# Delta rule of a two-layer network: the residual formed by VectorE per head, instead of by VectorE and GpSimd in turn

## The chip, the cores and the metric

The kernel runs on one core of one Trainium2 chip. The metric is the device time of one execution in microseconds (us). The kernel before took 2767.0 us, the median of 3 runs (2761.95 to 2785.57).

The engines' names in the profile: PE is TensorE's matmul, PEld its weight load, DVE is VectorE, ACT is ScalarE, POOL is GpSimd and SP is the engine that starts most transfers.

## The reference, cut to what matters

The network has two layers, each an attention block and a mixture of experts with adaptive layer norm. Only the attention block of the second layer is touched, a gated delta rule with 16 value heads of 64 by 64 over 8 sequences of 512 tokens:

```python
def step(S, xs):
    q_t, k_t, v_t, g_t, b_t = xs
    S = S * jnp.exp(g_t)[..., None, None]
    kv = jnp.einsum('bhk,bhkv->bhv', k_t, S)
    S = S + jnp.einsum('bhk,bhv->bhkv', k_t, (v_t - kv) * b_t[..., None])
    o_t = jnp.einsum('bhk,bhkv->bhv', q_t, S)
    return (S, o_t)
```

Ahead of it, q, k and v are projected, put through a causal convolution of 4 taps and a SiLU, and q and k are normalised. Behind it, the output is normalised per head, multiplied by silu(z) and projected.

## The kernel before, in words

The function delta1 computes the block in chunks of 32 tokens. The 128 partitions hold 4 sequences by 32 tokens, and the 8 sequences go in two passes of 16 chunks, so there are 32 steps k, and 16 pairs m of two steps (an even step e = 0, an odd step e = 1). The heads of a step are worked on in two halves f = 0 and 1, each a tile of 128 x 512 (8 heads by 64).

A step k does this, with the line and the engine of each part:

- read_out (PE, L2454): keys times state into the bank BK[f], then queries times state into BQ[f]. DVE scales BK[f] by the decay and key norm gk into Xs (L2086), and BQ[f] by the decay gT into O (L2092).
- residual (POOL, L1998): Xs becomes v - Xs, in place. The values vt come from PE (L2431) through ACT's SiLU (L2306).
- solve (PE, L2487): the triangular inverse Tt times Xs into BK[f]; ACT copies that to Ws (L2318).
- weigh (POOL, L2019): Ud is Ws times the decay to the chunk's end. add_state (PE, L2504): keys times Ud into BK. decay (POOL, L2010): the state S times its decay, one instruction for each f. update (DVE, L2189): S minus BK, two instructions for each f.
- attend (PE, L2518) and accumulate (DVE, L2195): O minus the weighted part of the chunk.

The signs are those of Tt and Pt, which are built from minus beta (d32 is minus the identity).

Beside that runs work for other chunks. For four steps ahead: the projection (PE, L2415), whose taps ACT makes (L2271, L2276, L2282: raw, the bank BY and yp) and DVE adds up (L2137, L2138, L2141), two times a step, as long as k is below 28. For the pair ahead: the norms (PE L2404, ACT L2257, DVE L2119 to L2132), POOL's diagonal Lt (L1992), DVE's scan L2149 and products L2156 and L2159 (even steps), and the forward substitution of the chunk's triangular system, 30 rows of a product (L2173) and a sum (L2174) on DVE, each chained to the one before through a semaphore, 11 of them in even steps and 19 in odd ones. For the step behind: the output's squares (ACT L2251, DVE L2099), the factor (DVE L2106 and L2107, ACT L2263, DVE L2112 and L2113), ACT's L2325, POOL's gate L2026, transposes and the output product (PE L2527, L2534).

Each engine's program is written out in a fixed order by hand, in a loop over k that runs the functions above one after another, and semaphores join them. Nothing is scheduled by a tool. DVE's order in a step is: squares, read_out of both halves, first convolution, squares, total, then in even steps norms and attend, in odd steps substitution; second convolution; and so on to accumulate and update of half 0, more substitution, and the same of half 1. POOL's order is: window, residual of both halves, diag (even steps), decay of half 0, diag (even), weigh of both halves, initial (even), decay of half 1, gated, halo.

decay(k, f) waits only for both of PE's read-outs of the step (the semaphore p_qs), and in the program stands behind the residuals:

```python
def decay(k, f):
    ...
    pool.wait_ge(s["p_qs"], half(k, 1))
```

Of the kernel before, what the change touches and what calls it, by code (L numbers as in the profile page):

```python
# [7 lines left out]
ALU = mybir.AluOpType  # L8
# [24 lines left out]
HV, HK, DK = 16, 8, 64  # L33
# [10 lines left out]
def bcast(ap, axis, n):  # L44

    a = [list(x) for x in ap.ap]
    a.insert(axis, [0, n])
    return bass.AP(ap.tensor, ap.offset, a)
# [1811 lines left out]
def delta1(nc, g, a):  # L1860

    PB, X, ident = g["PB"], g["X"], g["ident"]
    V, G = nc.vector, nc.gpsimd
    NS = 2 * NCK
    NP = NS // 2
    HF = HV // 2
    with ExitStack() as keep:
# [6 lines left out]
        Wqk, Wcv, Wz, Wo, cw, hT, bT, gT, GC = [w[n] for n in ("Wqk", "Wcv", "Wz", "Wo", "cw", "hT", "bT", "gT", "GC")]  # L1874
        with Stage(nc, ["p_ks", "p_qs", "p_w", "p_ds", "p_pu", "p_kk", "p_m",
                        "v_ks", "v_qs", "v_s", "v_o", "v_lt", "v_at", "v_ac", "v_tt", "v_conv", "v_ss",
                        "v_rn", "v_sr", "v_link", "g_x", "g_s", "g_d1", "g_t", "g_t0", "g_halo", "g_on", "g_hw", "g_ac", "v_nm", "a_kq", "g_ud",
                        "a_m", "a_w", "a_yp", "a_on", "a_sq", "a_osq", "a_or", "a_lk", "d_al0", "d_al1", "d_out"]) as s:
            raw = s.sb("raw", [P, 4, 2, 4, KS - 1 + 2 * CK])
            hw = s.sb("hw", [P, 2, KS, 4, CK])  # L1880
# [6 lines left out]
            gk = s.sb("gk", [P, 2, 2, HV])  # L1887
# [3 lines left out]
            vt = s.sb("vt", [P, 2, 512])  # L1891
            zs = s.sb("zs", [P, 2, 512])
            O = s.sb("O", [P, 2, 2, 512])
# [14 lines left out]
            Xs = s.sb("Xs", [P, 2, 512])  # L1908
# [5 lines left out]
            BK = (PB[3], PB[4])  # L1914
            BQ = (PB[5], PB[6])
            BY = PB[7]
            hd = lambda x: x.rearrange("p (h d) -> p h d", d=DK)
# [20 lines left out]
            done = lambda kind, x: USE[(kind, x)] + 1  # L1938
            half = lambda k, f: 2 * k + f + 1
            updates = lambda k, f: 2 * (k - k // NCK) + f + 1  # L1940

            with nc.Block() as block:
# [29 lines left out]
                def _(pool):  # L1972
# [5 lines left out]
                    def window(k):  # L1978
                        if k >= 2:
                            pool.wait_ge(s["p_m"], done("z", 2 * (k - 2) + 1))  # L1980
                        h = hb(k // NCK)
                        at = CK * (k % NCK)
                        last = None
                        for i in range(KS):
                            last = G.tensor_copy(hw[:, k % 2, i, :, :], h[:, :, at + i:at + i + CK])  # L1985
                        last.then_inc(s["g_hw"], 1)

                    def diag(c):
                        if c:
                            pool.wait_ge(s["v_at"], c)  # L1990
                        pool.wait_ge(s["v_nm"], c // 2 + 1)
                        G.tensor_tensor(Lt[:, :, :], bcast(bk[:, c % 2, :], 2, CK), bcast(w["d32"][:, :], 1, HV), ALU.mult)\  # L1992
                            .then_inc(s["g_d1"], 1)

                    def residual(k, f):
                        pool.wait_ge(s["v_ks"], half(k, f))
                        pool.wait_ge(s["a_m"], done("v", 2 * k + f))
                        G.tensor_tensor(Xs[:, f, :], vt[:, f, :], Xs[:, f, :], ALU.subtract).then_inc(s["g_x"], 1)  # L1998

                    def decay(k, f):  # L2000
                        if k == NS - 1:
                            return
                        pool.wait_ge(s["p_qs"], half(k, 1))
                        Sf = S[:, 2 * f:2 * f + 2, :, :]
                        if k % NCK == NCK - 1:
                            G.memset(Sf, 0.0).then_inc(s["g_s"], 1)
                        else:
                            gc = GC[:, k // NCK, k % NCK, 2 * f:2 * f + 2, :, :].rearrange("p x q v -> p (x q v)")
                            S3 = Sf.rearrange("p x q (v d) -> p (x q v) d", d=DK)
                            G.tensor_tensor(S3, S3, bcast(gc, 2, DK), ALU.mult).then_inc(s["g_s"], 1)  # L2010
# [11 lines left out]
                    def gated(k):  # L2022
                        for f in range(2):
                            pool.wait_ge(s["a_m"], done("z", 2 * k + f))
                            pool.wait_ge(s["a_on"], half(k, f))
                            G.tensor_tensor(O[:, k % 2, f, :], O[:, k % 2, f, :], zs[:, f, :], ALU.mult)\  # L2026
                                .then_inc(s["g_on"], 1)
# [24 lines left out]
                    for k in range(FIRST, LAST):  # L2052
                        m, e = k // 2, k % 2
                        if 0 <= k + 1 < NS:
                            window(k + 1)
                        if 0 <= k < NS:
                            residual(k, 0)
                            residual(k, 1)
                        if 0 <= m + 1 < NP and e == 0:
                            diag(2 * (m + 1))  # L2060
                        if 0 <= k < NS:
                            decay(k, 0)
                        if 0 <= m + 1 < NP and e == 0:
                            diag(2 * (m + 1) + 1)
                        if 0 <= k < NS:
                            weigh(k, 0)
                            weigh(k, 1)
                        if 0 <= m + 1 < NP and e == 0:
                            initial(m + 1)
                        if 0 <= k < NS:  # L2070
                            decay(k, 1)
                        if 0 <= k - 1 < NS:
                            gated(k - 1)
                        if (k + 4) // 2 < NP:
                            halo(2 * (k + 4))
                            halo(2 * (k + 4) + 1)

                @block.vector
                def _(dve):
                    link = linker(dve, s["v_link"])  # L2080

                    def read_out(k, f):
                        dve.wait_ge(s["p_ks"], half(k, f))
                        if k:
                            dve.wait_ge(s["p_w"], half(k - 1, f))
                        V.tensor_tensor(hd(Xs[:, f, :]), hd(BK[f][:, :]),  # L2086
                                        bcast(gk[:, k // 2 % 2, k % 2, HF * f:HF * f + HF], 2, DK), ALU.mult)\
                            .then_inc(s["v_ks"], 1)
                        dve.wait_ge(s["p_qs"], half(k, f))
                        if k >= 2:  # L2090
                            dve.wait_ge(s["p_m"], done("ot", 2 * (k - 2) + f))
                        V.tensor_tensor(hd(O[:, k % 2, f, :]), hd(BQ[f][:, :]), cols(gT, k, f), ALU.mult)\  # L2092
                            .then_inc(s["v_qs"], 1)
# [88 lines left out]
                    def update(k, f):  # L2182
                        if k % NCK == NCK - 1:
                            return
                        dve.wait_ge(s["p_ds"], updates(k, f))
                        dve.wait_ge(s["g_s"], half(k, f) + 2)
                        for x in (2 * f, 2 * f + 1):
                            Sx = S[:, x, :, :].rearrange("p q n -> p (q n)")
                            last = V.tensor_tensor(Sx, Sx, BK[x % 2][:, :], ALU.subtract)  # L2189
                        last.then_inc(s["v_s"], 1)  # L2190

                    def accumulate(k, f):
                        dve.wait_ge(s["p_pu"], half(k, f))
                        dve.wait_ge(s["v_qs"], half(k, f))
                        V.tensor_tensor(O[:, k % 2, f, :], O[:, k % 2, f, :], BQ[f][:, :], ALU.subtract)\  # L2195
                            .then_inc(s["v_o"], 1)

                    for k in range(FIRST, LAST):
# [6 lines left out]
                        if here:  # L2205
                            read_out(k, 0)
                            read_out(k, 1)
# [36 lines left out]
                def _(act):  # L2244
# [57 lines left out]
                    def values(k, f):  # L2302
                        act.wait_ge(s["p_m"], done("v", 2 * k + f))
                        if k:
                            act.wait_ge(s["g_x"], half(k - 1, f))
                        A_(vt[:, f, :], M[USE[("v", 2 * k + f)] % 2][:, :], ACT.Silu).then_inc(s["a_m"], 1)  # L2306

                    def gate(k, f):
# [76 lines left out]
                def _(pe):  # L2385
# [94 lines left out]
                    def solve(k, f):  # L2480
                        if k % 2 == 0 and f == 0:
                            pe.wait_ge(s["v_tt"], k // 2 + 1)
                        pe.wait_ge(s["g_x"], half(k, f))
                        for h in range(HF):
                            for x in range(4):
                                rows = slice(CK * x, CK * x + CK)
                                last = mm(BK[f][rows, DK * h:DK * h + DK], Tt[rows, :, k % 2, HF * f + h],  # L2487
                                          Xs[rows, f, DK * h:DK * h + DK], start=True, stop=True,
                                          tile_position=(CK * x, CK * x))
                        last.then_inc(s["p_w"], 1)  # L2490
# [118 lines left out]
```

## Time and profile before

| what | value |
| --- | --- |
| median of 3 runs | 2767.0 us (2761.95 to 2785.57) |
| the profiled execution | 2778.46 us |
| its span, first to last instruction | 2776.8 us |
| steps of the delta rule within it | about 1239 to 2324 us |
| busy over the span | PE 2194.6 us (79%), DVE 1890.6 (68%), ACT 1435.8 (52%), POOL 769.1 (28%) |
| mean granted TensorE clock | 0.854 |

A timeline row reads: start in us, duration in us, engine, line, operation, output <- inputs, shape, count, and in brackets how long the engine had been idle before it and what ended that. Rows that stand together on an engine are merged, with their count (x4) and the time from the first start to the last end. A row of the groups by line has busy us, mean ns of one, and the idle time before them. The share of busy time over the span says little here, since the stages have different limits; what counts for the change is the stretch of the delta rule.

### The profile page before, as it was taken

How to read it: one execution, taken by the hardware profiler on the slowest of the kernel's cores; microseconds unless marked ns; L12 is line 12 of the kernel's file. 1: busy time of each engine (PE TensorE's matmuls, PEld its weight loads, DVE VectorE, ACT ScalarE, POOL GpSimd, SP SyncE). 2: the span in 40 equal slices, each digit the busy share in tenths (PEclk: the TensorE clock that was granted, in tenths of full speed). 3: DMA queues.
4: the chain of work that ended last, by engine and by line, in shares of the span. 5: the costliest groups of instructions: out<-in, count | busy, mean ns of one | idle time of the engine just before them, and what ended most of it. 6: DMA issues, size and time to landing. Idle time of an engine off the chain costs nothing. (4 is left out here: it accounts for less than half of the span.)

```text
span 2776.8 us, 63709 instructions
## 1 busy us (share of the span) xinstructions
PE 2194.6 (79%) x25656; PEld 1388.4 (50%) x25656; DVE 1890.6 (68%) x4429; ACT 1435.8 (52%) x2901; POOL 769.1 (28%) x845
## 2 busy tenths in 40 slices
PE   2698888889888493468888888888888886587984
PEld 1244444444444282146666666666666664365552
DVE  2477677777766325568888898888888883673433
ACT  0376667667666221255666666666666644132321
POOL 1000001000010141024444444344444442202884
PEclk8599899999887796668888988888888888597997
DMA  5000000000000042200000000000000000433334
GB/s 187 26 1 5 5 5 9 5 5 8 5 7 6 25 117 53 65 9 11 12 12 12 12 12 12 12 12 11 11 12 12 4 4 6 139 110 91 53 43 86
DMA packets 109526, 85.53 MB, mean 31 GB/s; under 512 B 22366, under 2 KB 97282, under 8 KB 108976
## 3 DMA queue, kind: packets, MB, share of 16 engines
q1 hardware_dynamic: 95664, 68.31, 8.4%
q0 software_dynamic: 13568, 13.14, 2.9%
q8 instruction: 203, 3.33, 0.5%
q14 instruction: 91, 0.75, 0.1%
HBM read 59.22 MB, written 22.71 MB: 30 GB/s over the span
## 5 line engine op out<-in xcount | busy, mean ns | idle before, releaser
L617 ACT ACTIVATE Pr<-Pr,nmax 128x512 f32<-128x512 f32 x512 | 341.2, 714 | 177.4 <-DVE nmax L552 175.3
L722 PE MATMUL bank<-ident,Pr 128*128 128x128 f32 x2048 | 315.5, 297 | 71.6 <-DVE PT L561 59.8
L722 PEld LDWEIGHTS bank<-ident,Pr 128*128 128x128 f32 x2048 | 242.1, 151 | 258.8 <-DVE PT L561 157.2
L552 DVE CUSTOM_DVE_ANT_0 Pr<-bank,Tb 128x512 f32<-128x512 f32 x512 | 331.0, 684 | 42.4 <-PE bank L708 42.3
L561 DVE COPY PT<-bank 128x512 f32<-128x512 f32 x256 | 176.4, 689 | 188.2 <-PE bank L736 184.0
L2431 PE MATMUL bank<-Wcv,hw 128*128 128x512 f32 x512 | 265.1, 665 | 8.8 <-POOL hw L1985 5.3
L2173 DVE TENSOR_TENSOR pr<-AC,Tc 128x30 f32<-128x30 f32 (+14 forms) x480 | 214.9, 448 | 16.9 <-POOL Tc L2049 3.6
L624 ACT ACTIVATE PT<-bank 128x512 f32<-128x512 f32 x256 | 151.0, 590 | 112.9 <-PE bank L736 83.3
L2174 DVE TENSOR_TENSOR Tc<-Tc,pr 128x30 f32<-128x30 f32 (+14 forms) x480 | 178.8, 373 | 16.5
L708 PE MATMUL bank<-kp,qp 8*128 8x512 f32 x1024 | 178.4, 696 | 1.1 <-DVE nmax L552 1.1
L2431 PEld LDWEIGHTS bank<-Wcv,hw 128*128 128x128 f32 x512 | 103.5, 214 | 125.8 <-issue 118.0
L2282 ACT ACTIVATE yp<-raw,cwq 128x256 f32<-128x256 f32 x384 | 160.1, 510 | 0.0
L736 PE MATMUL bank<-PT,vp 128*9 128x512 f32 x1024 | 154.4, 676 | 0.0
L1998 POOL TENSOR_TENSOR Xs<-vt,Xs 128x512 f32<-128x512 f32 x64 | 80.6, 1275 | 243.7 <-DVE Xs L2086 243.6
L432 POOL DMA_INDIRECT disp<-H,slot x32 | 31.9, 995 | 396.8 <-DVE slot L508 389.5
L423 POOL TENSOR_SCALAR H<-X,rs,nm 128x128 f32<-128x128 f32 x32 | 14.0, 454 | 412.7 <-DVE nm L540 412.7
L2325 ACT ACTIVATE O<-O,nrm 128x64 f32<-128x64 f32 x512 | 125.4, 335 | 4.1 <-DVE nrm L2113 3.9
L2504 PE MATMUL bank<-Ud,Kt 32*64 32x128 f32 x1920 | 74.1, 296 | 56.1 <-DVE S L2189 51.7
L2487 PE MATMUL bank<-Xs,Tt 32*32 32x64 f32 x4096 | 88.5, 246 | 34.4 <-POOL Xs L1998 34.3
L2010 POOL TENSOR_TENSOR S<-S,GC 128x1024 f32<-128x1024 f32 x60 | 114.4, 1907 | 0.0
L1507 POOL DMA_INDIRECT acc<-eo,ids x64 | 101.0, 1578 | 40.6 <-issue 18.6
L2318 ACT ACTIVATE Ws<-bank 128x512 f32<-128x512 f32 x64 | 38.1, 596 | 139.9 <-PE bank L2487 139.8
(398 smaller groups left out, 4533.6 us busy)
## 6 DMA issues: line engine op xcount, KB each, us to landing
aB<-alpha SPq DMA_DIRECT2D x64, 128.0 KB, 2.7
Tb<-scores SPq DMA_DIRECT2D x1, 7168.0 KB
w<-in_L_ffn_W SPq DMA_DIRECT2D x16, 256.0 KB, 5.2
rawW<-in_L_ffn_up_w SPq DMA_DIRECT2D x16, 256.0 KB, 3.1
rawW<-in_L_ffn_gw SPq DMA_DIRECT2D x16, 256.0 KB, 3.5
rawW<-in_L_ffn_down_w SPq DMA_DIRECT2D x16, 256.0 KB, 4.0
disp<-zero SPq DMA_DIRECT2D x1, 2580.0 KB, 15.5
xin<-disp SPq DMA_DIRECT2D x8, 322.5 KB, 6.3
```

What stands on the lines that cost most here:

```text
L552: V.tensor_tensor_reduce(out=Pr[:, s, i, :], in0=pS[hh][:, :], in1=Tb[:, h, at:at + L], scale=-1.0, scalar=3.0e38, op0=ALU.add, op1=ALU.mi ...
L561: V.tensor_copy(PT[:, m % NPS, :], pT[m % 2][:, :]).then_inc(r["b_evd"], 1)
L617: A_(Pr[:, s, i, :], Pr[:, s, i, :], ACT.Exp, scale=-1.0, bias=nmax[:, s, i:i + 1])\
L624: A_(PT[:, m % NPS, :], pT[m % 2][:, :], ACT.Copy).then_inc(r["b_eva"], 1)
L708: mm(pS[hh][:, :], qp[rows, G % SLOTS, i * P:(i + 1) * P], kp[rows, G % SLOTS, :], start=True, stop=True, tile_position=(32 * hh, 0)).then ...
L722: last = TR(pT[m % 2][:, t * P:(t + 1) * P], Pr[:, (G % 2) * HG + hh, t, j * P:(j + 1) * P], ident[:, :])
L736: mm(pO[32 * hh:32 * hh + HD0 + 1, :], vp[:, b % 2, j, G % NG * HG + hh, :], PT[:, m % NPS, :], start=(j == 0), stop=(j == LT - 1), tile_p ...
L2173: link(V.tensor_tensor(o, bcast(AC[:, i + 1:CK, i], 2, i), bcast(Tc[:, i, 0:i], 1, n), ALU.mult))
L2174: link(V.tensor_tensor(Tc[:, i + 1:CK, 0:i], Tc[:, i + 1:CK, 0:i], o, ALU.add))
L2282: last = A_(yp[:, i, j, :, :], raw[:, tp, j, :, i:i + 2 * CK], ACT.Copy, scale=tap(j, i))
L2325: last = A_(of, of, ACT.Copy, scale=nrm[:, k % 2, HF * f + h:HF * f + h + 1])
L2431: last = mm(o[:, :], tokens(k, i), Wcv[:, i, 512 * f:512 * f + 512], start=(i == 0), stop=(i == KS - 1))
```

## The change

Before, the residual takes two operations on two engines: DVE's product of BK[f] and gk (128x512, gk broadcast along the 64 elements of each head), then POOL's difference v - Xs. After, DVE does both at once with scalar_tensor_tensor, whose scalar is one value per partition. Since the factor gk differs from head to head, each half takes 8 such instructions of 128x64. They form gk * BK - v, minus the former residual, so the two places that subtracted what follows from it (L2189 and L2195) now add. POOL's function and its semaphore g_x go; ACT's values and PE's solve wait for v_ks in its place, and DVE waits for the values before it starts.

```diff
-                    def residual(k, f):
-                        pool.wait_ge(s["v_ks"], half(k, f))
-                        pool.wait_ge(s["a_m"], done("v", 2 * k + f))
-                        G.tensor_tensor(Xs[:, f, :], vt[:, f, :], Xs[:, f, :], ALU.subtract).then_inc(s["g_x"], 1)
-
...
-                        if 0 <= k < NS:
-                            residual(k, 0)
-                            residual(k, 1)
...
-                        V.tensor_tensor(hd(Xs[:, f, :]), hd(BK[f][:, :]),
-                                        bcast(gk[:, k // 2 % 2, k % 2, HF * f:HF * f + HF], 2, DK), ALU.mult)\
-                            .then_inc(s["v_ks"], 1)
+                        dve.wait_ge(s["a_m"], done("v", 2 * k + f))
+                        for h in range(HF):
+                            of = slice(DK * h, DK * h + DK)
+                            last = V.scalar_tensor_tensor(Xs[:, f, of], BK[f][:, of],
+                                                          gk[:, k // 2 % 2, k % 2, HF * f + h:HF * f + h + 1],
+                                                          vt[:, f, of], ALU.mult, ALU.subtract)
+                        last.then_inc(s["v_ks"], 1)
...
-                            last = V.tensor_tensor(Sx, Sx, BK[x % 2][:, :], ALU.subtract)
+                            last = V.tensor_tensor(Sx, Sx, BK[x % 2][:, :], ALU.add)
...
-                        V.tensor_tensor(O[:, k % 2, f, :], O[:, k % 2, f, :], BQ[f][:, :], ALU.subtract)\
+                        V.tensor_tensor(O[:, k % 2, f, :], O[:, k % 2, f, :], BQ[f][:, :], ALU.add)\
...
-                            act.wait_ge(s["g_x"], half(k - 1, f))
+                            act.wait_ge(s["v_ks"], half(k - 1, f))
...
-                        pe.wait_ge(s["g_x"], half(k, f))
+                        pe.wait_ge(s["v_ks"], half(k, f))
```

The order on DVE in an odd step, before, from the squares' reduction ahead of read_out to the first convolution behind it (nrm holds the squares' sums, bank is here BK or BQ, and BY in the last row):

```order
1993 L2099 TENSOR_REDUCE nrm<-osq 128x8
1994 L2086 TENSOR_TENSOR Xs<-bank,gk 128x512
1995 L2092 TENSOR_TENSOR O<-bank,gT 128x512
1996 L2086 TENSOR_TENSOR Xs<-bank,gk 128x512
1997 L2092 TENSOR_TENSOR O<-bank,gT 128x512
1998 L2137 TENSOR_TENSOR bank<-bank,yp 128x512
```

The same place on DVE after the change:

```order
1993 L2095 TENSOR_REDUCE nrm<-osq 128x8
1994 L2081 SCALAR_TENSOR_TENSOR Xs<-bank,gk,vt 128x64 x8
1995 L2088 TENSOR_TENSOR O<-bank,gT 128x512
1996 L2081 SCALAR_TENSOR_TENSOR Xs<-bank,gk,vt 128x64 x8
1997 L2088 TENSOR_TENSOR O<-bank,gT 128x512
1998 L2133 TENSOR_TENSOR bank<-bank,yp 128x512
```

Nothing else changes its place on DVE; each L2086 has become 8 instructions. PE's and ACT's orders are as before.

The order on GpSimd in the same odd step, before: the window of the next step (hw), the residuals (Xs), decay of half 0 (S), weigh (Ud), decay of half 1, gate (O).

```order
146 L1985 COPY hw<-hTa 128x128 x4
147 L1998 TENSOR_TENSOR Xs<-vt,Xs 128x512 x2
148 L2010 TENSOR_TENSOR S<-S,GC 128x1024
149 L2019 TENSOR_TENSOR Ud<-Ws,dl 128x512 x2
150 L2010 TENSOR_TENSOR S<-S,GC 128x1024
151 L2026 TENSOR_TENSOR O<-O,zs 128x512 x2
```

The same place on GpSimd after the change:

```order
141 L1985 COPY hw<-hTa 128x128 x4
142 L2005 TENSOR_TENSOR S<-S,GC 128x1024
143 L2014 TENSOR_TENSOR Ud<-Ws,dl 128x512 x2
144 L2005 TENSOR_TENSOR S<-S,GC 128x1024
145 L2021 TENSOR_TENSOR O<-O,zs 128x512 x2
```

The decay of half 0 now stands directly behind the window. In an even step the diagonal Lt (L1992), which waits for DVE's norms, stands between the two, before and after.

## Rows read from the trace of the kernel before

**Rows 1.** Stretches: length, busy PE, PEld, DVE, ACT, POOL; PEclk, DMA share, GB/s.
```profile
1579.09:1605.68 26.59, 24.05 (x368) 17.79 (x368) 23.84 (x49) 16.28 (x41) 10.61 (x13) 0.87 0.02 5
...
1646.20:1677.36 31.16, 28.82 (x368) 21.26 (x368) 24.18 (x50) 16.32 (x41) 11.25 (x14) 0.73 0.02 4
1677.36:1717.82 40.46, 33.56 (x801) 22.59 (x800) 38.74 (x72) 30.37 (x73) 18.32 (x19) 1.00 0.06 17
1717.82:1748.93 31.11, 28.81 (x368) 21.29 (x368) 24.19 (x50) 16.30 (x41) 11.60 (x14) 0.73 0.02 4
```

**Rows 2.** Waits of DVE, 1239 to 2324 us: total us, times, longest.
```profile
DVE bank L2137 <- ACT yp L2282: 42.0, 14, 3.2
DVE rkq L2119 <- ACT rkq L2257: 22.2, 14, 2.8
```

**Rows 3.** Timeline of an odd step, from the read-out on.
```profile
1696.44 3.31 PE L2454 MATMUL bank<-S,kq 64*32 64x128 f32 x128
...
1700.74 0.68 DVE L2086 TENSOR_TENSOR Xs<-bank,gk 128x512 f32<-128x512 f32 x1
1701.34 0.68 DVE L2092 TENSOR_TENSOR O<-bank,gT 128x512 f32<-128x512 f32 x1
1701.50 2.50 POOL L1998 TENSOR_TENSOR Xs<-vt,Xs 128x512 f32<-128x512 f32 x2 [8.67 <-DVE Xs L2086]
...
1702.82 1.14 PE L2487 MATMUL bank<-Xs,Tt 32*32 32x64 f32 x64 [2.01 <-POOL Xs L1998]
...
1703.95 1.92 POOL L2010 TENSOR_TENSOR S<-S,GC 128x1024 f32<-128x1024 f32 x1
...
1705.31 0.81 ACT L2276 ACTIVATE bank<-bank,cwq 128x256 f32<-128x256 f32 x2 [0.20 <-DVE yc L2141]
...
1705.81 1.06 POOL L2019 TENSOR_TENSOR Ud<-Ws,dl 128x512 f32<-128x512 f32 x1
1705.91 0.98 DVE L2106 TENSOR_TENSOR rq<-rkq 128x8 f32<-128x8 f32 x1
...
1706.93 0.17 DVE L2107 TENSOR_TENSOR nrm<-nrm,rq 128x16 f32<-128x16 f32 x1
```

**Rows 4.** The same odd step's second half.
```profile
1713.63 1.91 POOL L2010 TENSOR_TENSOR S<-S,GC 128x1024 f32<-128x1024 f32 x1
...
1714.63 0.94 DVE L2113 TENSOR_TENSOR nrm<-nrm,rkq 128x16 f32<-128x16 f32 x1
...
1717.82 1.28 DVE L2189 TENSOR_TENSOR S<-S,bank 128x512 f32<-128x512 f32 x2
...
1719.24 1.98 PE L2504 MATMUL bank<-Ud,Kt 32*64 32x128 f32 x32 [3.38 <-DVE S L2189]
```

**Rows 5.** The even step behind it.
```profile
1731.77 0.69 DVE L2086 TENSOR_TENSOR Xs<-bank,gk 128x512 f32<-128x512 f32 x1
...
1737.39 0.17 DVE L2106 TENSOR_TENSOR rq<-rkq 128x8 f32<-128x8 f32 x1
...
1739.19 0.35 DVE L2119 RECIPROCAL rkq<-rkq 128x32 f32<-128x32 f32 x1 [1.43 <-ACT rkq L2257]
...
1741.11 1.90 POOL L2010 TENSOR_TENSOR S<-S,GC 128x1024 f32<-128x1024 f32 x1
1741.19 2.90 DVE L2149 TENSOR_TENSOR_SCAN Lt<-aB,Lt 128x512 f32<-128x512 f32 x1 [0.98 <-POOL Lt L1992]
...
1742.70 1.94 PE L2487 MATMUL bank<-Xs,Tt 32*32 32x64 f32 x64
...
1748.93 0.70 DVE L2137 TENSOR_TENSOR bank<-bank,yp 128x512 f32<-128x512 f32 x1 [3.17 <-ACT yp L2282]
```

**Rows 6.** scalar_tensor_tensor elsewhere: two groups by line.
```profile
L1631 DVE SCALAR_TENSOR_TENSOR hid<-bank,biasT,sg 128x512 f32<-128x512 f32 x64 | 48.0, 750 | 55.7 <-PE bank L1554 55.7
L1128 DVE SCALAR_TENSOR_TENSOR Y<-Y,factor,gbr 128x128 f32<-128x128 f32 x32 | 9.1, 344 | 11.4 <-DMA Y<-y 11.4
```

**Rows 7.** Timeline: four of L1128 in a row.
```profile
1065.22 1.14 DVE L1128 SCALAR_TENSOR_TENSOR Y<-Y,factor,gbr 128x128 f32<-128x128 f32 x4 [11.38 <-DMA Y<-y]
```

More of the change, by code:

```diff
@@ L1876, in delta1 @@
                         "v_ks", "v_qs", "v_s", "v_o", "v_lt", "v_at", "v_ac", "v_tt", "v_conv", "v_ss",
-                        "v_rn", "v_sr", "v_link", "g_x", "g_s", "g_d1", "g_t", "g_t0", "g_halo", "g_on", "g_hw", "g_ac", "v_nm", "a_kq", "g_ud",
+                        "v_rn", "v_sr", "v_link", "g_s", "g_d1", "g_t", "g_t0", "g_halo", "g_on", "g_hw", "g_ac", "v_nm", "a_kq", "g_ud",
                         "a_m", "a_w", "a_yp", "a_on", "a_sq", "a_osq", "a_or", "a_lk", "d_al0", "d_al1", "d_out"]) as s:
```

## The prediction

> **What bounds the kernel now.** I read four views: busy time by stretch, the waits of VectorE (DVE), the timeline of one pair of steps, and the groups by line for durations. The change touches only the delta rule, 32 steps k = 0 to 31 between 1239 and 2324 us. Its work repeats with a period of two steps: an even step carries the attention part (L2119 to L2164), an odd one most of the substitution.
>
> The busy time by stretch [rows 1] splits one period in two. From 1677.36 to 1717.82, from the second convolution of an even step to the first state update of the odd one, DVE is busy 38.74 of 40.46 us, and the gaps of 0.04 us between its chained operations (1705.91 + 0.98 to 1706.93, [rows 3]), some 40 of them, fill the rest: it waits for nobody. From 1717.82 to 1748.93 (31.11 us) DVE is busy only 24.19 us, while TensorE (PE) is busy 28.81. There the path runs over PE: the last row of [rows 4] shows PE waiting 3.38 us for the state update L2189, and then PE hardly stops through keys, gates, output, read-out, norms, similarities and solve, until ScalarE (ACT) has made yp. DVE waits for that at L2137, 3.17 us [rows 5]. Over the loop, DVE's waits [rows 2] are 42.0 us in 14 waits for yp (3.0 on average at a longest of 3.2, so nearly all periods are alike) and 22.2 in 14 for the roots (L2119).
>
> So the cycle is 40.5 us of DVE work plus some 31 us of PE work. What DVE gets more of in the first part is paid in full, in the second it is free up to its waits. The odd step's read_out (1700.74, [rows 3]) lies in the first part, the even step's (1731.77) in the second.
>
> **What the change adds: eight small operations for one.** Before, L2086 takes 0.68 us, and the next operation starts 0.60 after it [rows 3]. No row shows a 128x64 scalar_tensor_tensor from PSUM. Two rows bound it [rows 6, 7]: L1631, the same operation on 512 elements from PSUM, takes 750 ns, and L1128, on 128 elements from SBUF, 344. That is (750 - 344) / 384 = 1.06 ns an element, so 64 elements take 344 - 68 = 0.28 us. Four L1128 in a row span 1.14 us [rows 7], so their starts are (1.14 - 0.344) / 3 = 0.265 apart; less 64 elements that is 0.20 us. The lower end of the cost is then 8 x 0.20 = 1.60 against 0.60, +1.0 us per half and +2.0 per step. The upper end is no overlap at all, 0.32 us each with the 0.04 that stands between chained operations: 2.56 against 0.60, +2.0 per half and +3.9 per step. I take the lower, because four operations of this very kind, with their scalar read from memory, overlap in L1128's row.
>
> The Trainium skill, "VectorE: DVE Perf Modes", section "The DRAIN you can't avoid", says the next Vector operation does not start until the pipe has emptied, which would give the upper end. The trace disagrees where nothing holds the operation (starts 0.60 apart at 0.68 us each), and the page allows for that itself.
>
> **Even steps: hidden.** The 2.0 us fall between read_out and L2119, where DVE waits for the roots, 1.43 us in this period and 22.2 / 14 = 1.6 on average. The rest, about 0.5, goes into the 3.17 us wait for yp. Neither of these two arrivals depends on the read-out's DVE part: solve(k, 0) starts at 1742.70 [rows 5], and Xs is ready 8 us before. Cost 0; if that cover were gone it would be 2.0 us a step.
>
> **Odd steps: paid.** The first convolution L2137 starts 2.0 us later. That also moves ACT, whose L2276 waits for its result (1705.31, [rows 3]), and through yp, the table loads and Ws it moves GpSimd's weigh(k, 1) and decay(k, 1) by 2.0.
>
> **What the change removes.** GpSimd's L1998, 2 x 1.25 us a step. It ran next to DVE operations that read PSUM, and these were not slowed (0.68 us each), so its own time was free. What waited for it was PE's solve(k, 0), at 1702.82 after 2.01 us. The new Xs is ready at 1700.74 + 7 x 0.20 + 0.28 = 1702.42, against 1702.82: 0.3 to 0.4 us earlier, but PE then waits for DVE's L2189 anyway, so this is worth nothing. What is late next there is DVE itself.
>
> **Who meets whom.** DVE operations with two SBUF inputs stand still while GpSimd works: L2106, two inputs of 8 elements, takes 0.98 us beside GpSimd's L2019 (1705.81) and 0.17 in the even step [rows 3, 5]; the scan L2149 takes 2.90 beside decay. Without the residual, decay(k, 0) of an odd step starts when PE's read-out ends (1696.44 + 3.31 = 1699.75) instead of at 1703.95, and lies beside a reduction and the new operations. Weigh(k, 0) starts at about 1704.3, beside PSUM operations. So L2106's 0.81 us go. But decay of half 1, at 1713.63 [rows 4], moves by 2.0 with weigh ahead of it, where DVE would have moved only by 1.2: decay then covers 1715.65 to 1717.55, and L2113, which reads two SBUF tiles, comes at 1715.83 instead of after half of decay is over. It would take 1.7 us instead of the 0.94 of [rows 4], and the 0.8 are lost again. Net: +2.0 us for an odd step.
>
> **The sum.** 14 odd steps (k = 1 to 27) by 2.0 = 28, and two (k = 29, 31), where no convolution is left and DVE is not full, at 1 each: +30 us. The profiled execution took 2778.46 us (span 2776.8); it would become 2808.5. It lies 11.5 above the median of the three runs, 2767.0, so against the median I forecast 2797 us (+1.1%).
>
> **Rivals.**
>
> 1. *Part of it comes back.* Should L2113 not meet decay(k, 1), because ACT catches up, an odd step costs 1.2: 14 x 1.2 + 2 = 19 us. PE's stretch depends also on the clock: 31.16 and 31.11 us at 0.73 granted, but 26.59 at 0.87 [rows 1], levels of 1.2 and 2.4 GHz mixed. The periods so far vary with that, and shifting the pattern by 2 us may give more short stretches. One such in each four periods would give 4.5 x 3.5 = 16 back. For it: rows of both kinds exist. Against it: the waits for yp [rows 2] are nearly all alike. Time 2782 (+8 to +22 us).
>
> 2. *The clock turns it round: faster.* If the changed rhythm held the clock near 0.87 in every PE stretch, that stretch would shrink to DVE's own work. That is 31.11 - 3.17 - 1.43 = 26.5 us, plus the read-out's 2.0: 28.5, so 2.6 us less per period, against 2.0 more. 14 x (-0.6) is -9 us; with L2113 free as well it is 14 x (-1.4) = -20 us: 2750. It decides from a mean stretch below 29.1 us. For it speaks only the one short stretch of [rows 1]; against it, that PE idles no less than before in the DVE stretch.
>
> 3. *The new operations stand still beside decay.* They read PSUM, one SBUF tile and a scalar from SBUF. If the scalar counts as a second SBUF input, those of half 0 wait for decay(k, 0) to end, about 1.3 us after read_out starts: 14 x 3.3 + 2 = +48 us, 2815. The Trainium skill, "GPSIMD Engine Reference", section "Specifications", names two SBUF inputs (or a 2-port mode) as what contends with GpSimd; the stalled L2106 and L2149 agree, and whether a scalar counts it doesn't say. No row has this operation beside GpSimd's arithmetic.
>
> 4. *No overlap.* At 3.9 us a step the odd ones cost 14 x 3.9 + 2 = 57 us, 2824; even steps still hide it in 1.5 + 3.17.
>
> That the change doesn't do what it says is no rival: the order shows GpSimd without the subtraction and DVE with 8 operations at each of 64 places.
>
> **How the numbers follow.** Forecast 0.44 (its own range 2790 to 2804); rival 1 0.26; rival 2 0.08; rival 3 0.12; rival 4 0.10. A measurement tells about 1% from no change, here 27.7 us, so the line is at 2794.7. Of the forecast's case two thirds lie above it, a third below; rivals 3 and 4 are slower; rival 1 is within; of rival 2 a third or so would be faster by over 1%. Slower 0.29 + 0.22 = 0.51, same 0.15 + 0.26 + 0.05 = 0.46, faster 0.03. The range goes from inside rival 1 to rival 4: 2774 to 2828.
>
> **What would show it.** Right: the 8 operations span 1.7 us, and starts within are 0.20 apart; the DVE stretch of a period becomes 42.5; the even step's wait for the roots is near 0 and the one for yp stays above 2 us; L2106 near 0.17 in odd steps, and L2113 near 1.7; GpSimd 80 us less busy. Wrong: starts 0.3 apart (rival 4); a first new operation of over 1 us in odd steps (rival 3); a DVE stretch under 42 (the meeting with decay); PE stretches whose mean is not near 31 (rival 1 or 2).

## The result, and the profile after

The changed kernel takes 2807.22 us, the median of 4 runs (2801.45 to 2814.16), against 2770.49 us for the kernel before (4 runs). The ratio is 1.0109, with a 95% interval of 1.0074 to 1.0143: about 30 us slower by the ratio, 37 by the medians, where 2797 us (+30) was forecast. In the profiled executions, of which the one after is the lowest of its four, the difference is smaller: 2801.45 against 2778.46 us (span 2799.7 against 2776.8, +22.9). Each execution has its own pattern of the granted TensorE clock, as shown below.

The busy time by engine, from the page of the profile after:

```profile
PE 2200.4 (79%) x25656; PEld 1396.3 (50%) x25656; DVE 1937.1 (69%) x4877; ACT 1434.9 (51%) x2901; POOL 691.4 (25%) x781
```

POOL is 78 us less busy than before, DVE only 47 us more. Its Xs operations, 448 instructions more, take 103.5 us instead of 43.5, and the rest of its groups together some 13 us less.

The odd step that answers to [rows 3] and [rows 4], from the timeline:

```profile
1705.53 2.00 POOL L2005 TENSOR_TENSOR S<-S,GC 128x1024 f32<-128x1024 f32 x1 [7.04 <-PE bank L2450]
...
1706.41 1.62 DVE L2081 SCALAR_TENSOR_TENSOR Xs<-bank,gk,vt 128x64 f32<-128x64 f32 x8
...
1707.95 0.68 DVE L2088 TENSOR_TENSOR O<-bank,gT 128x512 f32<-128x512 f32 x1
...
1708.09 1.63 PE L2483 MATMUL bank<-Xs,Tt 32*32 32x64 f32 x64 [1.60 <-DVE Xs L2081]
1708.54 1.62 DVE L2081 SCALAR_TENSOR_TENSOR Xs<-bank,gk,vt 128x64 f32<-128x64 f32 x8
...
1710.67 0.69 DVE L2133 TENSOR_TENSOR bank<-bank,yp 128x512 f32<-128x512 f32 x1
...
1712.86 0.81 ACT L2272 ACTIVATE bank<-bank,cwq 128x256 f32<-128x256 f32 x2 [2.00 <-DVE yc L2137]
1713.45 0.17 DVE L2102 TENSOR_TENSOR rq<-rkq 128x8 f32<-128x8 f32 x1
...
1720.17 1.04 POOL L2014 TENSOR_TENSOR Ud<-Ws,dl 128x512 f32<-128x512 f32 x1 [8.70 <-ACT Ws L2314]
...
1721.18 1.90 POOL L2005 TENSOR_TENSOR S<-S,GC 128x1024 f32<-128x1024 f32 x1
...
1721.36 1.75 DVE L2109 TENSOR_TENSOR nrm<-nrm,rkq 128x16 f32<-128x16 f32 x1
```

Eight operations span 1.62 us, and the first convolution comes 4.26 us after the read-out's start (1706.41 to 1710.67). Decay now starts at 1705.53, right behind PE's read-out, and lies over the first eight. L2102 takes 0.17 us, where it had taken 0.98 [rows 3]; L2109 takes 1.75 beside the second decay, where it had taken 0.94 [rows 4].

The stretches that answer to [rows 1] (length; busy PE, PEld, DVE, ACT, POOL; granted clock): a PE stretch, the DVE stretch behind it, the next PE stretch.

```profile
1655.26:1683.02 27.76, 25.26 (x367) 18.74 (x368) 25.07 (x63) 15.55 (x39) 7.14 (x11) 0.82 0.02 5
1683.02:1725.36 42.34, 35.55 (x802) 23.48 (x800) 40.62 (x86) 30.99 (x76) 17.45 (x20) 0.96 0.05 16
1725.36:1756.88 31.52, 28.98 (x366) 21.93 (x367) 25.32 (x63) 15.54 (x39) 9.07 (x12) 0.68 0.02 4
```

The DVE stretch has grown from 40.46 to 42.34 us, and DVE is still busy through it; over 12 periods its mean went from 40.58 to 42.48. The PE stretches alternate: in the 12 periods between steps 1 and 27 in which both ends can be read, four last about 28 us and eight 31.4 to 31.6. Their mean, 30.3 us, is next to the 30.5 of the same periods before.

The even step behind it, which answers to [rows 5]:

```profile
1738.98 1.63 DVE L2081 SCALAR_TENSOR_TENSOR Xs<-bank,gk,vt 128x64 f32<-128x64 f32 x8 [0.32 <-PE bank L2450]
1741.12 1.62 DVE L2081 SCALAR_TENSOR_TENSOR Xs<-bank,gk,vt 128x64 f32<-128x64 f32 x8
...
1747.15 0.35 DVE L2115 RECIPROCAL rkq<-rkq 128x32 f32<-128x32 f32 x1 [0.74 <-ACT rkq L2253]
...
1750.66 1.94 PE L2483 MATMUL bank<-Xs,Tt 32*32 32x64 f32 x64
...
1756.88 0.70 DVE L2133 TENSOR_TENSOR bank<-bank,yp 128x512 f32<-128x512 f32 x1 [3.16 <-ACT yp L2278]
```

The read-out is 1.9 us longer here too. The wait for the roots takes up 0.7 of it (1.43 to 0.74). Some 0.3 go because the read-out comes sooner behind the odd step's state update (13.62 us instead of 13.95), and the stretch is 0.4 longer, at a granted clock of 0.68 instead of 0.73. The wait for yp is whole. Over the loop, the waits that answer to [rows 2]:

```profile
DVE bank L2133 <- ACT yp L2278: 31.6, 13, 3.2
...
DVE rkq L2115 <- ACT rkq L2253: 6.6, 9, 1.7
```

22.2 us for the roots have become 6.6, and 42.0 for yp 31.6. The two waits are 26 us less, where DVE got 14 x 1.9 = 26.6 us more work in the even steps. That the two agree so well is partly chance: in the eight long PE stretches the wait for yp is whole (3.16 us each, as before), and most of what is gone of it is gone in the four short ones, where it is 0.7 to 1.3 us, as it was 0.78 in the one of 26.59 us before [rows 1].

Where the loop's time went, from step starts (the first Xs operation of each step): from step 0 to step 31 it took 1107.45 us against 1083.54, +23.9. The 14 odd steps from 1 to 27 are 23.2 us longer, the 13 even ones from 2 to 26 2.2, steps 28 to 30 together 2.8, and step 0 is 4.2 shorter. Of the odd steps' 23.2, step 15 has 4.3 alone. It is the last of the first pass and has no state update. 2.4 us of it are waits for ACT and PE that the profile before does not have there, and that even_only's has without any change in that step. The other 13 are 1.46 us longer each, in four parts:

| part of an odd step, mean of 13 | before | after |
| --- | --- | --- |
| read-out to first convolution | 2.39 | 4.26 |
| to the second convolution (with L2106's meeting) | 9.15 | 8.34 |
| to the state update (with L2113's meeting) | 5.61 | 6.35 |
| to the even step's read-out | 13.86 | 13.52 |

In the last part GpSimd's gate of O meets fewer substitution rows, which take some 0.4 us each when nothing holds them. These are the ones that it stretches, two before and one after:

```profile
1719.01 0.89 DVE L2173 TENSOR_TENSOR pr<-AC,Tc 128x220 f32<-128x220 f32 x1
...
1720.36 1.44 DVE L2173 TENSOR_TENSOR pr<-AC,Tc 128x210 f32<-128x210 f32 x1
```

```profile
1727.39 1.33 DVE L2169 TENSOR_TENSOR pr<-AC,Tc 128x210 f32<-128x210 f32 x1
```

That is 0.6 us less. In the long PE stretches the read-out behind them then waits some 0.3 us for PE, as at 1738.98 above.

One profile shows one execution, and its share outside the loop varies too: in the twelve profiles step 0 starts between 1234 and 1250 us. Small differences of loop times between profiles are therefore not read as effects.

### The profile page after: what moved, and what is told of

Same layout as the page of the kernel before. It is cut to its first block and busy times, and to the rows that moved or that the text cites. A ratio compares the mean times of both kernels' runs of the same rounds, so it can differ in the third digit from the quotient of the medians.

```text
span 2799.7 us, 64031 instructions
## 1 busy us (share of the span) xinstructions
PE 2200.4 (79%) x25656; PEld 1396.3 (50%) x25656; DVE 1937.1 (69%) x4877; ACT 1434.9 (51%) x2901; POOL 691.4 (25%) x781
## 5 line engine op out<-in xcount | busy, mean ns | idle before, releaser
L2169 DVE TENSOR_TENSOR pr<-AC,Tc 128x30 f32<-128x30 f32 (+14 forms) x480 | 204.9, 427 | 17.1 <-POOL Tc L2044 3.8
L2500 PE MATMUL bank<-Ud,Kt 32*64 32x128 f32 x1920 | 79.9, 312 | 79.8 <-DVE S L2185 52.6
L2500 PEld LDWEIGHTS bank<-Ud,Kt 32*64 32x64 f32 x1920 | 63.5, 153 | 107.9 <-issue 69.9
L2014 POOL TENSOR_TENSOR Ud<-Ws,dl 128x512 f32<-128x512 f32 x60 | 63.2, 1054 | 215.8 <-ACT Ws L2314 215.8
L2450 PE MATMUL bank<-S,kq 64*32 64x128 f32 x4096 | 108.3, 274 | 2.2 <-DVE S L2185 2.2
```

The source lines that it names most:

```text
L2169: link(V.tensor_tensor(o, bcast(AC[:, i + 1:CK, i], 2, i), bcast(Tc[:, i, 0:i], 1, n), ALU.mult))
L2500: last = mm(BK[x % 2][64 * r:64 * r + 64, P * q:P * q + P], Kt[rows, k % 2, P * q + 64 * r:P * q + 64 * r + 64], Ud[rows, r, P * q:P * q + ...
```

## The experiments

Ten kernels were run, and every ratio is to the kernel before, run on the same chips.

| run | ratio, 95% interval | median us |
| --- | --- | --- |
| odd_only | 1.0118 [1.0080, 1.0157] | 2805.07 |
| even_only | 1.0009 [0.9984, 1.0035] | 2775.84 |
| two_wide | 1.0094 [1.0064, 1.0124] | 2796.30 |
| after_gap | 1.0015 [0.9986, 1.0044] | 2774.30 |
| twice_odd | 1.0295 [1.0259, 1.0330] | 2859.17 |
| twice_even | 1.0150 [1.0115, 1.0184] | 2817.89 |
| before_moved | 0.9984 [0.9958, 1.0011] | 2770.51 |
| after_moved | 0.9983 [0.9961, 1.0006] | 2772.18 |
| before_placed | 0.9903 [0.9872, 0.9934] | 2742.09 |
| after_placed | 0.9933 [0.9907, 0.9959] | 2751.86 |

### The change in odd steps alone, and in even steps alone

```diff
-                        dve.wait_ge(s["a_m"], done("v", 2 * k + f))
-                        for h in range(HF):
+                        if fused(k):
+                            dve.wait_ge(s["a_m"], done("v", 2 * k + f))
+                            for h in range(HF):
...
+                        else:
+                            last = V.tensor_tensor(hd(Xs[:, f, :]), hd(BK[f][:, :]),
+                                                   bcast(gk[:, k // 2 % 2, k % 2, HF * f:HF * f + HF], 2, DK), ALU.mult)
```

The edit is shown against the changed kernel. fused(k) is k % 2 == 1 in odd_only and k % 2 == 0 in even_only; in the other steps GpSimd forms Xs - vt.

> The fused residual in odd steps only; even steps keep VectorE's product and GpSimd's difference. Theory (the odd step's read-out lies in VectorE's stretch, the even step's behind waits): nearly the whole cost of the change is here, +1.9 us in each of 14 odd steps and about 1 in two, +24 to +30 us (+0.9 to +1.1%). Rival A (VectorE's added time is paid in both parities alike): half of it, +14 us (+0.5%). The odd step's L2113 should still take 1.75 us, and its start-to-update time 18.95 us.

> The fused residual in even steps only. Theory: hidden behind the waits for the roots and for yp, which shrink together by about 2 us a step; 0 us, within 6. Rival A: +14 us (+0.5%). Rival B (the clock's pattern moves with any shift): a change of either sign with longer or shorter TensorE stretches.

odd_only is 1.0118, a little over the expected 1.1%, and even_only 1.0009: the whole cost is in the odd steps, none that can be told from nothing in the even ones. Rival A would have had both near 1.005, and the upper end of even_only's interval, 1.0035, leaves it out. In odd_only's trace the DVE stretch is 42.5 us on average, as with the whole change, and in even_only's 40.8, next to 40.6 before. The waits of DVE in even_only's trace:

```profile
DVE bank L2150 <- ACT yp L2295: 26.5, 12, 3.2
...
DVE rkq L2132 <- ACT rkq L2270: 1.8, 3, 0.6
```

### The eight operations written twice

The second eight go to the memory of the tile A2 (spare), at a time when nobody reads it. Par stands for 1 in twice_odd and 0 in twice_even.

```diff
+                        for h in range(HF if k % 2 == par else 0):
+                            of = slice(DK * h, DK * h + DK)
+                            last = V.scalar_tensor_tensor(spare[:, f, of], BK[f][:, of],
+                                                          gk[:, k // 2 % 2, k % 2, HF * f + h:HF * f + h + 1],
+                                                          vt[:, f, of], ALU.mult, ALU.subtract)
```

> The changed kernel, with the eight operations of each half written once more in odd steps, into a tile that nobody reads. 8 x 0.19 = 1.5 us more a half, 3.1 an odd step. Theory (odd steps pay in full): 14 x 3.1 = 43 us and up to 3 in the two last odd steps on top of the change, +70 to +80 us over before (+2.6 to +2.9%). Rival (a clock effect or a wait absorbs part): under +60 us.

> The same repetition in even steps only. Theory: the changed kernel's waits left in even steps, 6.6 us for the roots and 31.5 for yp over 14 steps or 2.7 a step, take most of the 3.1; only what exceeds them is paid, most where TensorE's stretch is short: 5 to 15 us on top of the change, +35 to +45 us over before. Rival A (both parities pay alike): +70 to +80 us, as in the odd steps.

twice_odd costs 2.95%, some 82 us, a little over its upper end: 52 us more than the change. Its DVE stretch is 45.5 us, 3.1 more than after the change, which accounts for 14 x 3.1 = 43 of the 52; up to 3 were expected in the last two odd steps, and the rest is not explained. twice_even costs 1.50%, some 42 us, 11 more than the change; its interval and the change's overlap. Its waits show why it costs anything:

```profile
DVE S L2191 <- PE bank L2506: 13.8, 10, 4.5
...
DVE bank L2139 <- ACT yp L2284: 2.6, 4, 1.0
```

The wait for yp, 42.0 us before and 31.6 after the change, is used up but for 2.6, and that for the roots is gone. The one for PE's bank at the state update has grown from 7.9 us before and 10.7 after the change to 13.8. No PE stretch of this run is below 30.0 us. This is one of the short ones, by engine, and the DVE rows at its end:

```profile
1960.70:1990.72 30.02, 25.86 (x368) 18.85 (x368) 28.04 (x80) 17.62 (x41) 6.86 (x10) 0.83 0.02 4
...
1989.19 1.02 DVE L2158 TENSOR_TENSOR A<-bank,Lt 128x512 f32<-128x512 f32 x1
1990.05 0.67 DVE L2161 TENSOR_TENSOR Pt<-bank,Lt 128x512 f32<-128x512 f32 x1
1990.64 0.16 DVE L2162 COPY dl<-Lt 128x16 f32<-128x16 f32 x1
1990.72 0.70 DVE L2139 TENSOR_TENSOR bank<-bank,yp 128x512 f32<-128x512 f32 x1
```

DVE no longer waits for yp: its own work has become the lower bound of the stretch. Six of the twelve last 30.0 to 30.2 us at a granted clock of 0.78 to 0.83, where the four short ones after the change last 27.8 to 28.4 at 0.78 to 0.82. Six times some 2 us are about the 11 that this run costs more. So how much an even step can take depends on the granted clock in it: the 5.0 us of this run (1.9 + 3.1) still leave a wait for yp in four of the six long stretches, none in the short ones.

### Two wide operations instead of eight narrow ones

```diff
+                        link(V.tensor_tensor(hd(BK[f][:, :]), hd(BK[f][:, :]),
+                                             bcast(gk[:, k // 2 % 2, k % 2, HF * f:HF * f + HF], 2, DK), ALU.mult))
+                        V.tensor_tensor(Xs[:, f, :], BK[f][:, :], vt[:, f, :], ALU.subtract).then_inc(s["v_ks"], 1)
```

> The residual on VectorE in all steps, but as two operations of 128x512 (product in place in the bank, then minus the values) in place of eight of 128x64. Theory (what costs is the fixed part of each instruction): from first start to the next operation 0.72 + 0.60 = 1.32 us a half against 1.52 to 1.55 for the eight, so odd steps are 0.4 us shorter than with the change, -6 us: about +18 to +24 us over before. Rival (the work of 512 elements, not the count, costs): as long as the eight or longer, +30 us or more.

The timeline has one half of a step thus:

```profile
1716.98 0.69 DVE L2079 TENSOR_TENSOR bank<-bank,gk 128x512 f32<-128x512 f32 x1
1717.70 0.69 DVE L2081 TENSOR_TENSOR Xs<-bank,vt 128x512 f32<-128x512 f32 x1
1718.31 0.68 DVE L2085 TENSOR_TENSOR O<-bank,gT 128x512 f32<-128x512 f32 x1
```

1.33 us from the first start to the next operation, against 1.54 for the eight (1706.41 to 1707.95). That is twice the elements in less time, so the eight pay above all for the fixed part of each instruction. The DVE stretch is 42.06 us on average, 0.42 less than after the change, as expected. The ratio, 1.0094 (26 us, or 24 by the medians, where 18 to 24 were expected), is below 1.0109, but the intervals overlap, so the gain is shown in the trace and not in the time.

### What decay stands beside, in odd steps

after_gap holds decay of half 1 in odd steps until the sum of substitution row 19 is done, the last DVE operation ahead of the accumulation.

```diff
+                        if f == 1 and k % 2 and k // 2 + 1 < NP:
+                            pool.wait_ge(s["v_gap"], k // 2 + 1)
```

> The changed kernel, in which GpSimd's decay of half 1 in odd steps waits until VectorE has passed the two substitution rows ahead of the accumulation, so that it runs beside operations that read PSUM. Theory (odd steps lose 1.58 us to the meeting of L2109 and decay): L2109 takes 0.17 us in odd steps, VectorE's stretch of a period falls from 42.4 to 40.8 us, and 14 x 1.6 = 22 us go: +4 to +12 us over before. Rival A (decay then stands in the way of other two-input rows): the stretch stays above 42, no gain. Rival B (TensorE's stretch grows as VectorE's shrinks): the stretch falls as said and the time does not.

1.0015, so with one wait on GpSimd the change costs nothing that can be told. The group by line answers to the 1.75 us of L2109:

```profile
L2111 DVE TENSOR_TENSOR nrm<-nrm,rkq 128x16 f32<-128x16 f32 x31 | 29.8, 960 | 1.1
```

960 ns on average against 1634 after the change: 0.17 in every odd step, and still 1.85 in the even ones. The DVE stretch is 40.83 us on average. This confirms the meeting that the prediction added to the odd step.

### Decay moved in even steps too

before_moved and after_moved add one move: in even steps decay of half 1 stands ahead of initial, which scales AC.

```diff
+                        if 0 <= k < NS and e == 0:
+                            decay(k, 1)
                         if 0 <= m + 1 < NP and e == 0:
                             initial(m + 1)
-                        if 0 <= k < NS:
+                        if 0 <= k < NS and e == 1:
                             decay(k, 1)
```

> The kernel before, with only GpSimd's decay of half 1 moved: in odd steps it waits until VectorE has passed the two substitution rows ahead of the accumulation, in even steps it stands ahead of the scaling of AC (L2044) instead of behind it. Theory (VectorE's two-input operations stand still beside GpSimd, and its stretch is paid in full): L2113 0.94 to 0.17 us in odd steps, the first substitution row of even steps from 1.68 to below 0.3; VectorE's stretch 40.5 to about 38.3 us; 14 x 2.2 = 31 us less, -25 to -32 us (-1.0%). Rival A (the meeting only moves to other operations): within 8 us of before. Rival B (TensorE's clock gives it back in its own stretch): VectorE's stretch falls, the time does not.

> The changed kernel with the same two moves of decay. Theory: as the changed kernel with the decay held in odd steps (about 0 against before), less 1.5 us in each of 14 even steps: -15 to -20 us against before, and 10 to 14 us slower than the kernel before with the same moves, since the fused residual's 1.9 us outweigh the 0.8 of L2106 that it frees. Rival: equal to that kernel or faster.

Both miss: 0.9984 and 0.9983, where 25 to 32 and 15 to 20 us less were expected. The mean DVE stretch of before_moved is 40.04 us instead of 38.3, and the timeline of an even step shows the new meeting:

```profile
1675.70 1.90 POOL L2012 TENSOR_TENSOR S<-S,GC 128x1024 f32<-128x1024 f32 x1
1675.80 1.83 DVE L2164 COPY dl<-Lt 128x16 f32<-128x16 f32 x1
1677.66 1.25 DVE L2168 STREAM_TRANSPOSE AC<-A 128x1024 f32<-128x1024 f32 x1
```

A copy of 16 elements with one input stands still for 1.67 us. I had counted only operations with two SBUF inputs. The Trainium skill, "GPSIMD Engine Reference", section "Specifications", names DVE instructions in a two-port mode beside those with two inputs, and "VectorE: DVE Perf Modes", section "The perf-mode tier table (the rule you actually need)", gives an fp32 SBUF copy such a mode: by that rule, of which the prediction named both halves and used only the two inputs, the trace agrees. This is rival A of before_moved, and the move was a wash. In after_moved the recorded rival came true as well: that kernel is no slower than before_moved (2772.18 against 2770.51 us), though 10 to 14 us were expected. Its DVE stretch is 0.9 us longer in the mean (40.9 against 40.0), but its PE stretch 0.8 shorter (29.3 against 30.1).

### Decay placed behind the copy

```diff
+                            if m + 1 < NP:
+                                pool.wait_ge(s["v_at"], 2 * (m + 1) + 2)
                             decay(k, 1)
```

> The kernel before with the decay of half 1 placed anew: in odd steps as in the run before_moved, in even steps ahead of the scaling of AC, but only once VectorE has passed the small copy dl, which stood still for 1.67 us beside decay in before_moved. Theory (VectorE's stretch is paid in full, and what counts is that nothing with SBUF inputs that can stand still runs beside decay): copy 0.16 us, L2113 at most 0.8 us in even steps instead of 1.85, the first substitution row 0.2; VectorE's stretch from 40.6 to 37.0 to 38.0 us, and 14 x 3 = 42 us less: -30 to -45 us against before (-1.1 to -1.6%). Rival A (the meeting moves on to another operation again): the stretch stays above 39. Rival B (TensorE's stretch grows, since the clock's pattern shifts): the stretch falls as said, but less than half of it is seen in the time.

> The changed kernel with the same placement. Theory: VectorE's stretch 38.0 to 39.0 us, 1.1 us more than the kernel before with this placement (1.9 for the fused residual less 0.8 for L2106, which it frees): -15 to -30 us against before, and 10 to 18 us slower than before_placed. Rival: no slower than before_placed, by more short stretches of TensorE.

before_placed is 0.9903, some 27 us faster than the kernel before, and the fastest kernel here: it has nothing of the change. Its even step:

```profile
1733.48 0.15 DVE L2166 COPY dl<-Lt 128x16 f32<-128x16 f32 x1
1733.67 1.25 DVE L2170 STREAM_TRANSPOSE AC<-A 128x1024 f32<-128x1024 f32 x1
1733.71 1.90 POOL L2012 TENSOR_TENSOR S<-S,GC 128x1024 f32<-128x1024 f32 x1 [0.43 <-DVE dl L2166]
1734.84 0.21 DVE L2118 RECIPROCAL nrm<-nrm 128x16 f32<-128x16 f32 x1
1735.08 0.56 DVE L2119 TENSOR_TENSOR nrm<-nrm,rkq 128x16 f32<-128x16 f32 x1
...
1737.12 1.28 DVE L2200 TENSOR_TENSOR S<-S,bank 128x512 f32<-128x512 f32 x2 [0.88 <-PE bank L2515]
...
1739.07 1.22 DVE L2179 TENSOR_TENSOR pr<-AC,Tc 128x30 f32<-128x30 f32 x1 [0.67 <-POOL Tc L2051]
```

The transpose and the reciprocal run beside decay unharmed. The gain is under the -30 to -45 us expected: DVE, come earlier, meets two waits that it had hardly had (0.88 and 0.67 us here, 1.5 to 2.0 together in every period but the first), and its mean stretch is 38.92 us and not 37 to 38. after_placed is 0.9933, with a stretch of 39.92: the fused residual still costs 1.0 us of it, near the 1.1 expected. Its PE stretches were short in its profile, 28.7 us on average against 30.2, so that its span is only 4 us longer. The medians differ by 9.8 us, where 10 to 18 were expected, and 10 of after_placed's 12 runs lie above the highest of before_placed's 6, all on one chip. The intervals of the two ratios overlap, so that the change is still slower under this placement is likely, and its size is open. In the profiles of both pairs, moved and placed, a shorter PE stretch gives back most of what the fused residual adds to the DVE stretch, or more. There is one profile of each kernel; whether the change brings this on, as rivals 1 and 2 of the prediction had it, or chance, is not shown.

## Why the prediction was right, point by point

- *The bound.* A cycle of DVE work paid in full and PE work with waits in it. odd_only (1.0118) against even_only (1.0009), and twice_odd against twice_even, show it.
- *The price of eight for one.* 0.28 us each and 0.20 between starts were read off the groups of L1631 and L1128. Measured: 0.275 and (1.62 - 0.275) / 7 = 0.19. A step's read-out is 1.87 us longer, and 2.0 was forecast. Rival 4 (no overlap) falls.
- *Even steps hidden.* In the time so it is (even_only). In the trace the cover is not as forecast: the roots' wait fell from 22.2 to 6.6 us and is still 0.2 to 0.9 in the long PE stretches, where near 0 was forecast, and the wait for yp, forecast to give 0.5, is whole there. In the short ones it is 0.7 to 1.3 us, below the 2 that the prediction named. The cover was taken as even over the periods; it is thinner where the PE stretch is short, of which the shortest was 26.59 us before, 27.76 after and 30.00 in twice_even.
- *Who meets whom.* Both numbers came as forecast: L2106's 0.98 to 0.17, and L2113's 0.94 to 1.75 (forecast 1.7). after_gap takes the second away alone and with it 1.65 us of the stretch. That rules out rival 1's first half for this kernel, but shows that it needs only one wait on GpSimd to come true.
- *Rival 3*, that the eight stand still beside decay. They take 1.62 us at 1706.41 beside decay and 1.62 at 1708.54 with GpSimd idle. A scalar operand from SBUF next to one SBUF tile does not count as a second input. The price of this rival was too high: by [rows 3] decay, from 1699.75 for 1.92 us, ends 0.9 us after the read-out starts, not 1.3.
- *The clock.* Rival 1's second half and rival 2 rested on the PE stretch. Short ones did become more frequent, four of twelve instead of one or two (26.59 us, and one of 29.11), but the others lengthened from about 31.2 to 31.5 us, and the mean moved by 0.2 us only. Over the twelve profiles that mean lies between 28.7 and 30.7 us, so that it stayed put here is partly luck. Which pattern a given rhythm brings was not foreseen and is not explained here.
- *The sum.* 14 x 2.0 + 2. In the profile, an odd step grows by 1.87 - 0.81 + 0.74 = 1.80 us up to the state update, and 0.34 come back behind it, where GpSimd's gate stretches one substitution row and no longer two. The prediction had nothing for that. So 13 odd steps give 13 x 1.46 = 19 us and not 26, and the total of 23.2 is reached only with step 15, whose waits the prediction did not foresee. The last steps were put in the wrong place: step 29 is not longer, and step 28 is by 2.6 us. It is not for lack of cover, since DVE still waits 1.65 us for the roots in it (2.75 before), and in odd_only, which leaves this step alone, it is 1.8 us longer too; the cause is open. That the two together give what was forecast for steps 29 and 31 is luck.

The mechanism is shown: what odd steps pay, what even steps hide, and the two meetings. That the total came out at the forecast's 30 us owes something to luck, as the parts above show, and it lies as close to the line of 27.7 us as the chances said.

## What to carry to other kernels

An operation moved to an engine costs its full length in the stretch where that engine sets the pace, and little where the engine waits anyway: odd_only and even_only differ by 1.1%. GpSimd's residual had cost nothing as far as the rows show, because it ran beside operations that read PSUM and ahead of a PE that waited for something else; no run tests this alone. Before fusing per head, count instructions: eight of 64 elements took 1.54 us where one of 512 takes 0.60. And ask of every GpSimd operation what VectorE does meanwhile: moving one decay beside PSUM reads, a transpose and a reciprocal was worth 1%.

## What the runs showed of the hardware that I had not expected

- A one-input copy of 16 elements from SBUF to SBUF stands still beside a GpSimd tensor_tensor (1.83 us instead of 0.15), while beside decay a reduction (0.69 us at 1705.81 after the change, 0.67 at 1712.74 without GpSimd), a stream transpose (1.25), a reciprocal (0.21) and the operations with one PSUM input (1.62 for eight) keep their time.
- It works the other way too: decay at 1705.53 takes 2.00 us instead of 1.90, and a DVE row of two inputs, started at 1705.39, is then under way. Of the seven decays of that profile that start while such a row is under way, six take 1.97 to 2.06 us; all others take 1.90 or 1.91.
- The granted clock of the DVE stretch differs between kernels: 0.96 to 1.00 before, 0.92 to 0.97 after, 0.89 to 0.96 in twice_odd, whose stretches last over 45 us (each without the first period). Length alone does not decide it, for before_moved has 0.92 at 41.0 us. DVE is busy through these stretches all the same.
